# Attention scores behind the band in every second pair of units, and three score banks used in plain rotation

## The chip, the cores and the metric

The kernel runs on one core of a Trainium2 chip. The metric is the device time of one execution in microseconds (us); before the change it is 1020.58 us, the median of three runs (1019.04 to 1022.09).

## The reference, cut to what matters

One transformer layer, 8 sequences of 512 tokens, width 256, 16 heads of 16, in fp32:

```python
x = x + attention(layernorm(x))       # below
x = x + moe(layernorm(x))             # 7 routed experts, top 2, and 1 shared

q, k, v = shape(h @ Wq.T), shape(h @ Wk.T), shape(h @ Wv.T)      # (8, 16, 512, 16)
scores = einsum('bhqd,bhkd->bhqk', q, k) * SCALING + position_bias
ctx = einsum('bhqk,bhkd->bhqd', softmax(scores), v)
out = ctx @ Wo.T
```

`position_bias[h, q, k]` depends on k - q alone, and is constant where |k - q| is at least 91.

## The kernel before, in words

Three stages follow one another: `project` (q, k, v and the bias to HBM), `attend`, and `finish` (output projection, router and experts). The change lies in `attend`.

`attend` walks through 32 slots. A slot is one sequence and a group of four heads, and has 8 steps; a step is one pair of heads (two sides, on the upper and the lower half of the contraction rows) and one tile of 128 positions. Three streams of work are laid over each other on TensorE in each step of slot n:

- `scores` (line 740, tile pS): two matmuls of 512 columns, one for each side, each into a bank of pS. Each is a "unit"; a slot has 16. They are made 15 steps ahead of the exponents (`LEAD` = 7, plus a slot), only to find the row maxima. VectorE (line 680) adds the bias `near` to a unit and reduces it to its negated maximum in one instruction, followed by a short read of the accumulator that raises the semaphore `max_done`. A unit's bank is free again when `max_done` has counted it.
- `exponents` (line 757, tile pE): the scores once more, transposed, with the negated maximum and far bias as extra contraction rows, two matmuls of 512 columns; then eight short matmuls (line 765) that add the bias band of 154 to 244 columns. ScalarE (line 711) takes the exponent of two banks at once. pE has four banks, so steps alternate between two halves.
- `values` (line 779, tile pC): in every odd step, eight fp32 matmuls of the slot before's probabilities with v; `copy_ctx` (line 719) empties pC on ScalarE once a slot.

After the 16 units of a slot, `turn` (lines 687, 689, 693) splits and transposes the maxima on VectorE; GpSimd then sends them to HBM and back into the rows of `q_st` (lines 642 and 649), where the exponents of that slot read them. SyncE loads q, k, v, the far rows and, at the start of a group, the bias.

The order on TensorE is written out by hand in `slot` of `attend`: in each step `scores`, then `exponents`, then in odd steps `values`. Scores made in step s of a slot are those of step (s + 7) mod 8 of a later one, so an even step makes the units of an odd step, and the other way round. Write a and b for the two units of an even step of a slot, c and d for those of the odd step behind it, and a', b' for the next ones. The four units of such a pair of steps are what "pair" means below.

Three of pS's banks are used. Units go to places, and place modulo 3 is the bank; two places of each 18 (those before unit 6 and before unit 14) are left empty (`PLACES`). So most units wait for the unit three before them (line 739), units 6, 7, 14 and 15 for the one two before them, and units 8 and 0 for the one five before them (`held`). In regular places, d waits for a, a' for b, b' for c and c' for d.

Of the kernel before, what the change touches and what calls it, by code (L numbers as in the profile page):

```python
# [18 lines left out]
P = 128  # L19
B, S, D = 8, 512, 256  # L20
# [13 lines left out]
BIG = 3.0e38  # L34
# [15 lines left out]
def band_start(kh):  # L50

    return S - 1 - (FAR - 1) - (HALF - 1) - HALF * kh


def band(kh):

    return max(0, band_start(kh)), min(S, band_start(kh) + BW)
# [15 lines left out]
def raw(t):  # L73

    return t.bitcast(F32)
# [450 lines left out]
def attend(nc, mk, g):  # L526
# [5 lines left out]
    near, bandT, q_st, k_st, v_raw = (g[n] for n in ("near", "bandT", "q_st", "k_st", "v_raw"))  # L532
    near_ld, band_ld, qk_ld, far_ld, v_ld = (g[n] for n in ("near_ld", "band_ld", "qk_ld", "far_ld", "v_ld"))
    passed = g["passed"]
    with ExitStack() as ctx:
# [3 lines left out]
        sums = sb("sums", [P, 4, S], BF16)  # L539
# [4 lines left out]
        pS = ps("pS", [P, 3, S], F32)  # L544
        pE = ps("pE", [P, 4, S], F32)
        pC = ps("pC", [P, S], F32)
        s_mm, max_done, split_done, max_turned, max_out, max_ld = (sem(n) for n in (
            "s_mm", "max_done", "split_done", "max_turned", "max_out", "max_loaded"))
# [3 lines left out]
        PV0, MAX0 = 8, 4  # L552
# [1 line left out]
        STEPS = HPG // 2 * TT  # L554
        LEAD = 7

        PLACES = [*range(6), None, *range(6, 14), None, 14, 15]
        BANK = {unit: k % 3 for k, unit in enumerate(PLACES)}

        def held(unit):  # L560

            k = PLACES.index(unit) - 3
            while PLACES[k] is None:
                k -= 3
            return PLACES[k] + 1 - (16 if k < 0 else 0)

        def await_stores(engine):

# [4 lines left out]
        with nc.Block() as block:  # L573
# [90 lines left out]
            @block.vector  # L664
            def _(dve):
                dve.sem_inc(max_done, MAX0)  # L666

                def maxima(m, step):

                    hg = m // 8  # L670
                    pair, t = divmod(step, TT)
                    for side in range(2):
                        j, r = 2 * pair + side, 2 * step + side
                        if m % 8 == 0 and t == 0:
                            dve.wait_ge(near_ld[j], 16 * (hg + 1))
                        unit = 16 * m + r
                        dve.wait_ge(s_mm, unit + 1)
                        dve.wait_ge(max_done, MAX0 + unit - 3)
                        lead = P * t
                        dve.tensor_tensor_reduce(sums[:, r % 4], pS[:, BANK[r]], near[:, hg % 2, j, lead:lead + S], -1.0, BIG,  # L680
                                                 ALU.add, ALU.min,
                                                 nmax[:, j, t:t + 1]).then_inc(max_done, 1)

                def turn(m):

                    dve.wait_ge(max_done, MAX0 + 16 * m + 16)
                    dve.tensor_copy(nparts[:, 0], nmax[:]).then_inc(split_done, 1)
                    dve.wait_ge(split_done, 2 * m + 1)
                    dve.tensor_tensor(nparts[:, 1], nmax[:], nparts[:, 0], ALU.subtract).then_inc(split_done, 1)
                    dve.wait_ge(split_done, 2 * m + 2)  # L690
                    if m >= 2:
                        dve.wait_ge(max_out, 16 * m - 16)
                    dve.transpose(turned[:, m % 2], raw(nparts[:].rearrange("p a j t -> p (a j t)"))).then_inc(max_turned, 1)

                for ahead in range(STEPS * NI):
                    m, step = divmod(ahead, STEPS)
                    maxima(m, step)
                    if step == STEPS - 1:
                        turn(m)
                dve.wait_ge(den_ld, 16)  # L700
                dve.reciprocal(den[:], den[:]).then_inc(den_inv, 1)
# [24 lines left out]
            @block.tensor  # L726
            def _(pe):
                pe.sem_inc(pv_done, PV0)
                pe.wait_ge(g["rows_set"], 32)

                def scores(m, r, rounds, step):

                    pair, t = divmod(step, TT)
                    if step == 0:
                        pe.wait_ge(qk_ld[r], 16 * 8 * rounds)
                    for side in range(2):
                        unit = 2 * step + side
                        rows = slice(HALF * side, HALF * side + KQ)
                        pe.wait_ge(max_done, MAX0 + 16 * m + held(unit))
                        pe.matmul(pS[:, BANK[unit]], q_st[rows, r, pair, P * t:P * t + P], k_st[rows, r, pair],  # L740
                                  start=True, stop=True).then_inc(s_mm, 1)

                def exponents(n, r, step, quad, u, first):

                    pair, t = divmod(step, TT)
                    if u == 0 and t == 0 and quad % 2 == 0:
                        for side in range(2):
                            pe.wait_ge(band_ld[2 * pair + side], 16 * (quad // 2 + 1))
                    if step == 0:
                        pe.wait_ge(far_ld[r], 32 * (quad // 2 + 1))  # L750
                        pe.wait_ge(max_ld, 32 * (n + 1))
                    if not (first and step < 2):
                        pe.wait_ge(exp_done, STEPS * n + step - 1)
                    bank = 2 * (step % 2)
                    for side in range(2):
                        rows = slice(HALF * side, HALF * side + KS)
                        pe.matmul(pE[:, bank + side], k_st[rows, r, pair, P * t:P * t + P], q_st[rows, r, pair],  # L757
                                  start=True, stop=False, skip_group_check=True)
                    for half in range(2):
                        a, z = band(2 * t + half)  # L760
                        lead = a - band_start(2 * t + half)
                        for part in range(2):
                            for side in range(2):
                                rows = slice(HALF * side, HALF * side + HALF)
                                ins = pe.matmul(pE[:, bank + side, a:z], place[rows, half],  # L765
                                                bandT[rows, (quad // 2) % 2, pair, part, lead:lead + z - a],
                                                start=False, stop=half == 1 and part == 1, skip_group_check=True)
                    ins.then_inc(e_mm, 1)

                def values(n, par, t, first=False):  # L770

                    if t == 0:
                        pe.wait_ge(exp_done, STEPS * n + STEPS)
                        pe.wait_ge(v_ready, n + 1)
                        if not first:
                            pe.wait_ge(evac, n)
                    for j in range(HPG):
                        at = 8 * (j // 2) + 2 * t + j % 2
                        ins = pe.matmul(pC[32 * j:32 * j + 32], v_aug[:, par, t, j], prob[:, par, at],  # L779
                                        start=t == 0, stop=t == TT - 1, skip_group_check=True)  # L780
                    ins.then_inc(pv_done, 1)

                def slot(n, u, quad, first=False, last=False):
                    for step in range(STEPS):
                        ahead, other = divmod(STEPS + step + LEAD, STEPS)
                        if not (last and u + ahead > 3):
                            scores(n + ahead, (u + ahead) % 4, quad + 1 + (u + ahead) // 4, other)
                        exponents(n, u, step, quad, u, first and u == 0)
                        if step % 2 == 1 and not (first and u == 0):
                            values(n - 1, (u + 1) % 2, step // 2, first and u == 1)  # L790

                for step in range(STEPS + LEAD):
                    scores(step // STEPS, step // STEPS, 1, step % STEPS)
                for quad in range(QUADS):
                    for u in range(4):
                        slot(4 * quad + u, u, quad, first=quad == 0, last=quad == QUADS - 1)
                for t in range(TT):
                    values(NI - 1, 1, t)
# [488 lines left out]
```

## Time and profile before

| | us |
|---|---|
| median of 3 runs | 1020.58 |
| the profiled execution | 1021.6 |
| its span in the trace | 1019.8 |
| of it, slots 1 to 29 of attention | 391.56 |

The profiled execution is 1.8 us longer than its span, and 1.0 us longer than the median. TensorE is busy 95% of the span, VectorE 69%, ScalarE 50%. How to read the rows: a timeline row gives the start and the length of a merged group of instructions and, in brackets, the idle time before it and who ended it. PE is the matmul side of TensorE, PEld its loads of stationary operands. A matmul's wait is carried by its load, so PEld rows show who held it. The start of a matmul is recorded, its end is modelled; so the argument goes by starts.

### The profile page before, as it was taken

The numbers are of one execution on the slowest core, as the hardware profiler recorded it, in microseconds if no ns is written. First come the engines' busy times: TensorE is split into PE (matmuls) and PEld (weight loads), VectorE is DVE, ScalarE is ACT, GpSimd is POOL, SyncE is SP. The second block draws the span as 40 slices with busy tenths as digits, with TensorE's granted clock in tenths as the row PEclk, the third lists the DMA queues.
The fourth block names the chain that finished last, engine by engine and source line by source line (L and its number), as shares of the span: only waits on it lengthen the run. The fifth ranks groups of instructions, "written<-read, shape, count | busy, mean of one in ns | idle before, by whom it ended". The sixth has DMA issues, their size and how long they took to land. (4 is left out here: it accounts for less than half of the span.)

```text
span 1019.8 us, 20280 instructions
## 1 busy us (share of the span) xinstructions
PE 966.6 (95%) x7264; PEld 721.1 (71%) x7264; DVE 703.4 (69%) x2048; ACT 514.8 (50%) x680; POOL 109.4 (11%) x245
## 2 busy tenths in 40 slices
PE   5799599999999999999999499999999999999998
PEld 3688266666666666666665388888888798888887
DVE  5575587777787877777781667666666575766664
ACT  2344046666666666666667355444344334434433
POOL 2111021111111111111111100000000000000000
PEclk9899589999999999999999699999999999999999
DMA  4998864334543444333352411101111110101000
GB/s 115 303 342 282 240 136 125 104 95 120 132 115 105 125 136 127 86 94 93 87 156 80 134 42 52 60 25 43 41 42 43 41 41 21 62 1 42 1 22 21
DMA packets 65715, 100.27 MB, mean 98 GB/s; under 512 B 11256, under 2 KB 39440, under 8 KB 65598
## 3 DMA queue, kind: packets, MB, share of 16 engines
q1 hardware_dynamic: 62386, 97.49, 31.8%
q0 software_dynamic: 3072, 1.11, 1.0%
q8 instruction: 51, 0.84, 0.4%
q10 hardware_dynamic: 172, 0.56, 0.2%
q14 instruction: 34, 0.28, 0.1%
HBM read 63.67 MB, written 34.93 MB: 97 GB/s over the span
## 5 line engine op out<-in xcount | busy, mean ns | idle before, releaser
L680 DVE CUSTOM_DVE_ANT_0 sums<-pS,near 128x512 bf16<-128x512 f32 x512 | 324.8, 686 | 91.0 <-PE pS L740 90.7
L711 ACT ACTIVATE prob<-pE 128x1024 f32<-128x1024 f32 x256 | 261.3, 1025 | 173.4 <-PE pE L765 173.0
L1187 PE MATMUL pD<-w2p,h_p 128*128 128x256 f32 x1536 | 203.0, 285 | 1.8 <-DVE x L1037 1.8
L1187 PEld LDWEIGHTS pD<-w2p,h_p 128*128 128x128 f32 x1536 | 191.4, 188 | 11.2 <-DVE x L1037 2.6
L765 PEld LDWEIGHTS pE<-bandT,place 64*128 64x128 f32 x2048 | 183.6, 188 | 16.4
L1169 PE MATMUL pU<-x2T,w1p 128*128 128x512 f32 x768 | 191.7, 399 | 0.0
L1100 ACT ACTIVATE h_f<-pU,b1s 128x512 f32<-128x512 f32 x128 | 88.1, 688 | 191.8 <-PE pU L1169 185.9
L740 PE MATMUL pS<-k_st,q_st 48*128 48x512 f32 x512 | 171.8, 493 | 11.5 <-DVEq L666 7.7
L765 PE MATMUL pE<-bandT,place 64*128 64x244 f32 (+2 forms) x2048 | 181.8, 270 | 0.0
L740 PEld LDWEIGHTS pS<-k_st,q_st 48*128 48x128 f32 x512 | 75.3, 191 | 142.3 <-DVE nmax L680 132.3
L1169 PEld LDWEIGHTS pU<-x2T,w1p 128*128 128x128 f32 x768 | 141.6, 190 | 29.5
L1037 DVE SCALAR_TENSOR_TENSOR x<-pD,combine,x 128x256 f32<-128x256 f32 x256 | 110.8, 478 | 64.0 <-PE pD L1187 62.4
L757 PE MATMUL pE<-q_st,k_st 62*128 62x512 f32 x512 | 142.6, 423 | 0.0
L779 PE MATMUL pC<-prob,v_aug 128*32 128x512 f32 x1024 | 135.7, 604 | 1.0 <-ACT ctx_sb L719 1.0
L1026 DVE TENSOR_TENSOR h_p<-h_f,h_p 128x512 fp32r<-128x512 f32 x128 | 86.8, 690 | 68.0 <-ACT h_p L1103 65.6
L1103 ACT ACTIVATE h_p<-pU,b1s 128x512 fp32r<-128x512 f32 x128 | 87.2, 681 | 0.0
L757 PEld LDWEIGHTS pE<-q_st,k_st 62*128 62x128 f32 x512 | 61.4, 187 | 6.2 <-ACT prob L711 5.0
L472 PE MATMUL pQ<-xT,w_p 128*128 128x512 f32 x192 | 51.3, 420 | 7.8 <-DVE qk L390 5.8
L472 PEld LDWEIGHTS pQ<-xT,w_p 128*128 128x128 f32 x192 | 37.4, 203 | 19.6 <-DVE qk L390 9.9
L214 POOL TENSOR_SCALAR rtmp<-mv 128x4 f32<-128x4 f32 x16 | 5.8, 364 | 422.8 <-DVE mv L946 359.1
L649 POOL DMA_DIRECT2D q_st<-negated_maxima x64 | 34.8, 548 | 83.5 <-DMA negated_maxima<-turned 83.5
L680 DVE DVE_READ_ACCUMULATOR2_ANT nmax<- 128x1 f32 x512 | 42.4, 83 | 0.0
(102 smaller groups left out, 575.4 us busy)
## 6 DMA issues: line engine op xcount, KB each, us to landing
x<-in_x SPq DMA_DIRECT2D x16, 512.0 KB, 4.4
q_parts<-qk SPq DMA_DIRECT2D x16, 512.0 KB, 5.0
k_parts<-qk SPq DMA_DIRECT2D x16, 512.0 KB, 4.6
q_st<-q_parts SPq DMA_DIRECT2D x64, 128.0 KB, 2.8
k_st<-k_parts SPq DMA_DIRECT2D x64, 128.0 KB, 2.9
ctx<-ctx_sb SPq DMA_DIRECT2D x32, 256.0 KB, 2.7
near<-bias_by_distance SPq DMA_DIRECT2D x16, 448.0 KB, 5.7
v_rows<-vs SPq DMA_DIRECT2D x8, 512.0 KB, 3.4
```

The source lines that it names most:

```text
L472: ins = pe.matmul(pQ[:, m % 2], w_p[:, a, w, c, P * h:P * h + P], xT[:, par, z, c], start=k == 0, stop=k == 5)
L680: dve.tensor_tensor_reduce(sums[:, r % 4], pS[:, BANK[r]], near[:, hg % 2, j, lead:lead + S], -1.0, BIG, ALU.add, ALU.min, nmax[:, j, t:t ...
L711: act.activation(prob[:, par, 2 * step:2 * step + 2], pE[:, 2 * (step % 2):2 * (step % 2) + 2], ACT.Exp).then_inc(exp_done, 1)
L740: pe.matmul(pS[:, BANK[unit]], q_st[rows, r, pair, P * t:P * t + P], k_st[rows, r, pair], start=True, stop=True).then_inc(s_mm, 1)
L757: pe.matmul(pE[:, bank + side], k_st[rows, r, pair, P * t:P * t + P], q_st[rows, r, pair], start=True, stop=False, skip_group_check=True)
L765: ins = pe.matmul(pE[:, bank + side, a:z], place[rows, half], bandT[rows, (quad // 2) % 2, pair, part, lead:lead + z - a], start=False, st ...
L779: ins = pe.matmul(pC[32 * j:32 * j + 32], v_aug[:, par, t, j], prob[:, par, at], start=t == 0, stop=t == TT - 1, skip_group_check=True)
L1037: dve.scalar_tensor_tensor(out=row, in0=pD[:, t // 2, t % 2], scalar=combine[:, par, t, e:e + 1], in1=row, op0=ALU.mult, op1=ALU.add).then ...
L1100: act.activation(h_f[:, e % 2, m], pU[:, e % 2, m], ACT.Gelu, bias=b1s[:, e, m:m + 1])
L1103: act.activation(h_p[:, e % 2, 0, m], pU[:, e % 2, m], ACT.Gelu, bias=b1s[:, e, m:m + 1]).then_inc(s["h_hi"], 1)
L1169: ins = pe.matmul(pU[:, e % 2, m], w1p[:, e, a, c, P * m:P * m + P], x2T[:, par, c, z], start=k == 0, stop=k == 5)
L1187: ins = pe.matmul(pD[:, t2, u], h_p[:, e % 2, a, m, P * t:P * t + P], w2p[:, e, z, m], start=k == 0 and e < NE - 1, stop=k == 5)
```

## The change

`PLACES`, `BANK` and `held` go: unit u counted through all slots lies in bank u modulo 3, and waits for unit u - 3, always. In odd steps `scores` is issued behind `exponents` (and ahead of `values`); even steps keep their order. The line numbers of the new kernel are 8 or so smaller below the removed lines. No instruction is added or removed apart from that.

```diff
-        PLACES = [*range(6), None, *range(6, 14), None, 14, 15]
-        BANK = {unit: k % 3 for k, unit in enumerate(PLACES)}
-
-        def held(unit):
-
-            k = PLACES.index(unit) - 3
-            while PLACES[k] is None:
-                k -= 3
-            return PLACES[k] + 1 - (16 if k < 0 else 0)
+        PS = 3
...
-                        dve.tensor_tensor_reduce(sums[:, r % 4], pS[:, BANK[r]], near[:, hg % 2, j, lead:lead + S], -1.0, BIG,
+                        dve.tensor_tensor_reduce(sums[:, r % 4], pS[:, unit % PS], near[:, hg % 2, j, lead:lead + S], -1.0, BIG,
...
-                        unit = 2 * step + side
+                        unit = 16 * m + 2 * step + side
                         rows = slice(HALF * side, HALF * side + KQ)
-                        pe.wait_ge(max_done, MAX0 + 16 * m + held(unit))
-                        pe.matmul(pS[:, BANK[unit]], q_st[rows, r, pair, P * t:P * t + P], k_st[rows, r, pair],
+                        pe.wait_ge(max_done, MAX0 + unit + 1 - PS)
+                        pe.matmul(pS[:, unit % PS], q_st[rows, r, pair, P * t:P * t + P], k_st[rows, r, pair],
                                   start=True, stop=True).then_inc(s_mm, 1)
...
-                        if not (last and u + ahead > 3):
+                        early = step % 2 == 0
+                        if early and not (last and u + ahead > 3):
                             scores(n + ahead, (u + ahead) % 4, quad + 1 + (u + ahead) // 4, other)
                         exponents(n, u, step, quad, u, first and u == 0)
+                        if not early and not (last and u + ahead > 3):
+                            scores(n + ahead, (u + ahead) % 4, quad + 1 + (u + ahead) // 4, other)
```

## Rows read from the trace of the kernel before

**Rows 1.** The page's first part: busy us (share of the span) xinstructions of each engine.

```profile
PE 966.6 (95%) x7264; PEld 721.1 (71%) x7264; DVE 703.4 (69%) x2048; ACT 514.8 (50%) x680; POOL 109.4 (11%) x245
```

**Rows 2.** Stretches: us, busy of PE, PEld, DVE, ACT, POOL, PEclk, DMA share, GB/s.

```profile
106.20:136.90 30.70, 21.85 (x56) 11.22 (x58) 22.43 (x74) 1.13 (x2) 4.10 (x7) 0.50 0.92 223
...
144.93:536.49 391.56, 391.56 (x3714) 245.34 (x3715) 309.90 (x1015) 254.89 (x262) 62.78 (x116) 1.00 0.41 114
...
563.60:590.90 27.30, 15.04 (x53) 11.26 (x54) 19.80 (x60) 9.48 (x16) 2.68 (x8) 0.56 0.43 126
```

**Rows 3.** Waits in 144.93 to 536.49: us in total, times, longest us.

```profile
PEld pS L740 <- DVE nmax L680: 118.6, 231, 0.8
```

**Rows 4.** Timeline of PE, one pair of steps in slot 12: start, us, instruction.

```profile
303.17 0.50 PE L740 MATMUL pS<-k_st,q_st 48*128 48x512 f32 x2
303.51 0.40 PE L757 MATMUL pE<-q_st,k_st 62*128 62x512 f32 x2
303.74 0.61 PE L765 MATMUL pE<-bandT,place 64*128 64x244 f32 x8
304.19 0.76 PE L740 MATMUL pS<-k_st,q_st 48*128 48x512 f32 x2
304.46 0.72 PE L757 MATMUL pE<-q_st,k_st 62*128 62x512 f32 x2
304.80 0.79 PE L765 MATMUL pE<-bandT,place 64*128 64x218 f32 x8
305.52 1.07 PE L779 MATMUL pC<-prob,v_aug 128*32 128x512 f32 x8
306.52 0.50 PE L740 MATMUL pS<-k_st,q_st 48*128 48x512 f32 x2
```

**Rows 5.** Timeline of PEld, the waiting loads of the same pair.

```profile
303.16 0.19 PEld L740 LDWEIGHTS pS<-k_st,q_st 48*128 48x128 f32 x2 [0.84 <-DVE nmax L680]
...
304.46 0.18 PEld L740 LDWEIGHTS pS<-k_st,q_st 48*128 48x128 f32 x1 [0.19 <-DVE nmax L680]
```

**Rows 6.** Timeline of DVE, the eviction of unit a of the same pair.

```profile
303.70 0.69 DVE L680 CUSTOM_DVE_ANT_0 sums<-pS,near 128x512 bf16<-128x512 f32 x1 [0.87 <-PE pS L740]
304.32 0.08 DVE L680 DVE_READ_ACCUMULATOR2_ANT nmax<- 128x1 f32 x1
```

**Rows 7.** Timeline of PE in slots 30 and 31, where scores run out.

```profile
536.15 0.50 PE L740 MATMUL pS<-k_st,q_st 48*128 48x512 f32 x2
536.49 0.40 PE L757 MATMUL pE<-q_st,k_st 62*128 62x512 f32 x2
...
538.95 0.50 PE L757 MATMUL pE<-q_st,k_st 62*128 62x512 f32 x2
...
541.47 0.50 PE L757 MATMUL pE<-q_st,k_st 62*128 62x512 f32 x2
...
551.63 0.50 PE L757 MATMUL pE<-q_st,k_st 62*128 62x512 f32 x2
...
554.20 0.50 PE L757 MATMUL pE<-q_st,k_st 62*128 62x512 f32 x2
```

**Rows 8.** Timeline of DVE around the turn of a slot: b ends, then c.

```profile
308.28 0.08 DVE L680 DVE_READ_ACCUMULATOR2_ANT nmax<- 128x1 f32 x1
...
308.95 0.68 DVE L680 CUSTOM_DVE_ANT_0 sums<-pS,near 128x512 bf16<-128x512 f32 x1
309.55 0.08 DVE L680 DVE_READ_ACCUMULATOR2_ANT nmax<- 128x1 f32 x1
```

**Rows 9.** Timeline of DVE in the lead, at a unit behind an empty place.

```profile
116.58 0.69 DVE L680 CUSTOM_DVE_ANT_0 sums<-pS,near 128x512 bf16<-128x512 f32 x1 [0.27 <-PE pS L740]
```

**Rows 10.** Timeline of PE, the first exponents of slot 0.

```profile
133.41 0.80 PE L757 MATMUL pE<-q_st,k_st 62*128 62x512 f32 x2
```

**Rows 11.** Timelines of POOL in slot 13 and SP in slot 15: maxima back, last load.

```profile
312.38 1.09 POOL L649 DMA_DIRECT2D q_st<-negated_maxima x2 [2.36 <-DMA negated_maxima<-turned]
...
338.45 0.35 SPq L200 DMA_DIRECT2D v_raw<-v_rows  x1
```

## The prediction, made before the change was run

> **What bounds the kernel now.** I read the page's busy times first, then the stretches by stage, then the waits of the attention stage, then the timelines of one pair of steps. The page says TensorE: 95% busy [rows 1]. The stretches put 391.56 us on slots 1 to 29 of attention, at the full clock (1.00, the 2.4 GHz level), with TensorE busy in every microsecond [rows 2]. That is 391.56 / 29 = 13.50 us a slot, 3.375 us a pair of steps. "Busy" is too kind, though: a matmul's end is modelled, and a row can cover a stall. The waits say that loads for pS stood idle for VectorE 118.6 us in 231 cases, two a pair [rows 3]. The timeline shows the two kinds. One is 0.84 us at the first scores of a pair, the other 0.19 us at unit d [rows 5].
>
> The 0.84 us one is no wait for VectorE. It spans the `values` matmuls, and stands in the same length where nothing can be waited for: from values to the next work is 306.52 - 305.52 = 1.00 us [rows 4], most of it the fp32 matmuls themselves. The 0.19 us one is real. Unit d needs the bank of a. Unit a's matmul starts at 303.17, its eviction at 303.70 (0.535 us later); the accumulator read that raises `max_done` starts at 304.32 and takes 0.083 us [rows 6]; d's load starts at 304.46 [rows 5]. So a bank comes back 0.535 + 0.616 + 0.083 + 0.055 = 1.29 us after its matmul when VectorE is free. But d could have run beside c at 304.19. While d is held, so are the exponents behind it in TensorE's order: exponents to band takes 304.80 - 304.46 = 0.34 us where the unheld one takes 303.74 - 303.51 = 0.23 us, the loads of the sides drift apart and no longer pair up, and values start only at 305.52 [rows 4].
>
> What would a pair cost without the stall? Slots 30 and 31 show it, since there scores run out. A pair without scores takes 541.47 - 538.95 = 2.52 us (long band, then short) or 554.20 - 551.63 = 2.57 us (short, then long), 2.545 on average [rows 7]. One pair of score matmuls costs 0.235 us: from the last scores to the next pair is 538.95 - 536.15 = 2.80 us, 0.23 above 2.57 [rows 7], the same as an unheld exponent pair [rows 4]. So 2.545 + 2 x 0.235 = 3.015 us a pair, 12.06 us a slot. The stall costs 3.375 - 3.015 = 0.36 us a pair.
>
> **The change part by part.** *Scores of odd steps behind the band.* No instruction is added; the work of c and d is 0.235 us in either place. Take a's matmul as 0. Even step: scores to exponents 0.34 (536.15 to 536.49) [rows 7], exponents and band 0.68 (303.51 to 304.19, the long band, the dearer one) [rows 4]; odd step the same at most, 0.68. So c and d now start at about 1.70 instead of 1.02, and a's bank is back at 1.29. The stall of d goes whole, with 0.4 us to spare. Whatever c and d are moved past is on TensorE itself: the exponents and band of the odd step come 0.235 us plus the stall earlier, so ScalarE gets that step earlier. It can take it: it is busy 254.89 / 29 = 8.8 us a slot [rows 2], of 12.2.
>
> *What is late next: b'.* b' needs the bank of c. c starts at 1.70, is evicted from 1.70 + 0.535, and its bank is back at 1.70 + 1.29 = 2.99. TensorE reaches a' and b' at 3.03 in such a pair (2.57 + 0.47); in the other (2.52) both shrink together. So b' finds its bank with 0.04 us to spare: no stall, but next to nothing in hand. a' needs b, back at about 1.90; c' needs d; d' needs a'. VectorE evicts one unit every 0.61 us (303.70 to 304.32) [rows 6], so 2.45 us a pair; a and b run 0.54 to 1.76, c and d 2.24 to 3.47, and a' is ready at 3.03 + 0.54 = 3.57. It keeps up, with 0.1 us of slack where it had 0.9.
>
> A rule of the Trainium skill speaks against that last step. VectorE: DVE Perf Modes, section "The DRAIN you can't avoid", says that a VectorE instruction's successor doesn't start before the pipe is empty, though it also lets those that are not held start earlier. The trace disagrees with the strict reading for this instruction: 0.69 us long, the next one 0.61 us behind it.
>
> *Regular banks.* The two empty places a slot go. Their units waited for the one two before them; that cost VectorE 0.27 us of idle time each in the lead, where scores run alone [rows 9]. In the 15 steps of the lead there are four such places: up to 4 x 0.27 = 1.1 us gained, or nothing where a load of q and k ends last there instead. The price is at the turn: it takes VectorE from 308.28 to 308.95, 0.67 us between b and c [rows 8]. c's eviction can then start at 1.76 + 0.67 = 2.43 instead of 2.24. The read is 0.60 later [rows 8], so b's successor b' gets its bank at 2.43 + 0.60 + 0.084 + 0.055 = 3.17 against 3.03: a stall of 0.14 us once a slot. Before, the wait for the unit five back kept c' out of this. Between nothing (if it is made up in the band) and 0.36 (if it upsets the pairing as d's 0.19 does now), I take 0.14, the plain delay.
>
> *Slot 0* has no values, so TensorE has only 2 us of work a pair there and the loop c to b' binds: 2.99 us a pair. It now takes from 133.41 [rows 10] to 144.93 [rows 2], 2.88 us a pair, so some 0.5 us more in sum. With the lead's gain I book nothing for the two, within 1 us. Part of it runs at the 1.2 GHz level (0.50 until 136.90) [rows 2]. Slots 30 and 31 have no scores to move.
>
> *Queues.* SyncE and GpSimd get no new order, only shorter slots. The reload of the maxima starts at 312.38 and takes 1.1 us to issue [rows 11]; it lands by about 316 and is wanted at the next slot's start, 320.0 now, 318.7 then. SyncE's last load of a slot is issued 5 us into it (338.45; the slot began at 333.5) [rows 11], and is wanted over a slot later. Neither ends last. `finish` is untouched; its start at the mixed clock (0.56) [rows 2] may move 2 us either way, as the clock's steps fall differently on it.
>
> **Sum.** A slot 4 x 3.015 + 0.14 = 12.20 us against 13.50: 1.30 x 29 = 37.7 us. Profiled execution 1021.6 - 37.7 = 983.9. The median of the runs stands 1.0 below the profiled one: 982.9, so 983.
>
> **The rivals.** *(1) The stall moves to b'.* The 0.04 us in hand is less than what I can read off sums of rows. If the loop closes 0.1 to 0.15 us late, or the disturbance costs double its wait as at d now, a pair takes about 3.14 us, a slot 12.7: 23 us gained, 997. For: the thin margin. Against: c's place was taken at the dearer band.
> *(2) VectorE becomes the bound.* If its real interval between units were the instruction and the read one after the other, 0.69 + 0.08 = 0.77 us, a pair would need 3.08 us and the turn 0.67 more a slot: 13.0 us, 15 us gained, 1005. Against: it keeps 0.61 in every row that I read. The Trainium skill's page named above, read strictly, would give this.
> *(3) Slower.* One mechanism: c issued late makes b' late on top of a stall that stays at d. It would be a pair of 3.015 + 2 x 0.36 = 3.73 us, a slot 14.9, 41 us lost: 1062. It decides from the point where c gives its bank back more than 0.4 us later than worked out (2.99 + 0.39 = 3.38), so that the new stall outweighs the old one; each 0.1 us beyond costs 11.6 us. Against: a's own bank comes back in 1.29 by row, and c's is the same work.
> *(4) It does nothing.* If the 0.36 us a pair is no stall but a cost of four score matmuls among the others, reordering leaves it: 1020. Against: the 0.19 us row and the drifting sides.
>
> **How the numbers follow.** Forecast 0.72; (1) 0.12; (2) 0.04; (4) 0.05; (3) 0.07. The forecast's own bounds: no cost of the turn (0.14 x 29 = 4 us), 1 us from the lead and 2 from the clock give 976; the turn at 0.36 and the clock against me give 992. To leave out no more than 2 in 10 the range reaches to the middle of rival 1 and a little past it: 976 to 1000. A difference of 0.3% (3 us) is about what a measurement of this kernel tells from no change. Faster: 0.72 + 0.12 + 0.04 = 0.88; same 0.05; slower 0.07.
>
> **What would show it right or wrong.** Right: slots of 12.2 us between 144 and 500; scores c and d as a row of two in one piece, 1.7 us after a and b, with values 0.33 us behind; no 0.19 us idle row at a pS load in the plain pair, and one of about 0.14 once a slot; exponent to band 0.23 us in odd steps. Rival 1: a short pS load wait in every pair, at its second load. Rival 2: VectorE without gaps. Wrong altogether: a slot still at 13.5 with no waiting load, or the exponents waiting for the maxima or for ScalarE at a slot's start.

## The result, and the profile after

The changed kernel takes 989.01 us, the median of four runs (985.09 to 991.38), against 1021.11 before (1019.04 to 1022.09, four runs): a ratio of 0.968, 95% interval 0.965 to 0.972. The forecast was 983 (976 to 1000), a ratio of 0.963. The profiled execution took 985.09, its span 983.3. No TensorE, VectorE or ScalarE instruction came or went; the page's busy line, which answers to [rows 1], shows 35.5 us of TensorE's "busy" gone, which in the main was stall under the modelled ends:

```profile
PE 931.1 (95%) x7264; PEld 695.4 (71%) x7264; DVE 708.1 (72%) x2048; ACT 501.3 (51%) x680; POOL 109.4 (11%) x245
```

The stretches of after (columns as in [rows 2]): the stretch at the low clock, slot 0, slots 1 to 29, and the start of `finish`.

```profile
106.63:140.76 34.13, 26.19 (x79) 14.58 (x79) 23.93 (x81) 3.79 (x4) 5.59 (x10) 0.50 0.78 205
...
132.62:146.38 13.76, 12.28 (x96) 10.05 (x97) 9.06 (x32) 7.57 (x8) 2.19 (x4) 0.70 0.31 83
...
146.38:502.20 355.82, 355.81 (x3713) 219.13 (x3715) 315.58 (x1016) 242.07 (x262) 62.79 (x116) 1.00 0.44 126
...
529.88:550.36 20.48, 9.88 (x38) 7.21 (x38) 14.09 (x30) 6.68 (x12) 2.62 (x6) 0.58 0.50 154
```

Slots 1 to 29 took 355.82 / 29 = 12.27 us each instead of 13.50: 35.7 us gained. The rest of the span: slot 0 began 0.8 us earlier (first exponents at 132.62, before 133.41), slot 0 took 13.76 us instead of 11.52 (2.2 lost), and what follows slot 29 took 983.3 - 502.20 = 481.1 instead of 1019.8 - 536.49 = 483.3 (2.2 gained; `finish` started with 20.48 us at 0.58 of the full clock, where [rows 2] has 27.30 at 0.56). Sum 36.5 = 1019.8 - 983.3.

One plain pair of after on TensorE (timeline, slot 14), to be laid beside [rows 4]:

```profile
311.71 0.50 PE L732 MATMUL pS<-k_st,q_st 48*128 48x512 f32 x2
312.05 0.40 PE L749 MATMUL pE<-q_st,k_st 62*128 62x512 f32 x2
312.28 0.60 PE L757 MATMUL pE<-bandT,place 64*128 64x154 f32 x8
312.72 0.41 PE L749 MATMUL pE<-q_st,k_st 62*128 62x512 f32 x2
312.96 0.62 PE L757 MATMUL pE<-bandT,place 64*128 64x244 f32 x8
313.42 0.39 PE L732 MATMUL pS<-k_st,q_st 48*128 48x512 f32 x2
313.74 1.07 PE L771 MATMUL pC<-prob,v_aug 128*32 128x512 f32 x8
314.74 0.50 PE L732 MATMUL pS<-k_st,q_st 48*128 48x512 f32 x2
```

Both exponents now run to their band in 0.23 to 0.24 us, where the second one took 0.34 before; c and d start at 313.42, 1.71 us behind a and b; values follow 0.32 us later; the pair takes 3.03 us. The weight loads of the same stretch (PEld, in brackets the idle time before), and VectorE at c:

```profile
308.51 0.36 PEld L732 LDWEIGHTS pS<-k_st,q_st 48*128 48x128 f32 x2 [0.84 <-issue]
...
311.71 0.19 PEld L732 LDWEIGHTS pS<-k_st,q_st 48*128 48x128 f32 x2 [0.84 <-DVE nmax L672]
...
313.31 0.19 PEld L732 LDWEIGHTS pS<-k_st,q_st 48*128 48x128 f32 x2
...
314.73 0.19 PEld L732 LDWEIGHTS pS<-k_st,q_st 48*128 48x128 f32 x2 [0.84 <-DVE nmax L672]
```

```profile
313.94 0.69 DVE L672 CUSTOM_DVE_ANT_0 sums<-pS,near 128x512 bf16<-128x512 f32 x1 [0.39 <-issue]
314.56 0.08 DVE L672 DVE_READ_ACCUMULATOR2_ANT nmax<- 128x1 f32 x1
```

The 0.19 us wait of [rows 5] is gone from c and d (313.31, no bracket). c's accumulator read ends at 314.56 + 0.08 = 314.64, and the loads of a' and b' go at 314.73: b' had its bank about 0.04 us before it was wanted, once the 0.055 us from semaphore to load is counted. The 0.84 us brackets stay, as they must: they span the values. The row at 308.51 is the other case, the turn. It covers two loads in 0.36 us instead of 0.19: b' went 0.18 us after a'. VectorE says why; its turn ended so late that c was evicted from 307.94 and read at 308.55, and b's successor could not load before 308.69. Of the 29 turns, 24 have such a row of 0.32 to 0.34 us, so about 0.15 us of delay; three have 0.18, one 0.10, and one, at 480, has 0.50, behind an eviction for whose start the trace names no releaser. VectorE at the turn of 308:

```profile
307.94 0.69 DVE L672 CUSTOM_DVE_ANT_0 sums<-pS,near 128x512 bf16<-128x512 f32 x1
308.55 0.08 DVE L672 DVE_READ_ACCUMULATOR2_ANT nmax<- 128x1 f32 x1
```

### The profile page after: what moved, and what is told of

Read it like the earlier page. It is cut to its first block and busy times, and to the rows that moved or that the text cites. A ratio compares the mean times of both kernels' runs of the same rounds, so it can differ in the third digit from the quotient of the medians.

```text
span 983.3 us, 20280 instructions
## 1 busy us (share of the span) xinstructions
PE 931.1 (95%) x7264; PEld 695.4 (71%) x7264; DVE 708.1 (72%) x2048; ACT 501.3 (51%) x680; POOL 109.4 (11%) x245
## 5 line engine op out<-in xcount | busy, mean ns | idle before, releaser
L672 DVE CUSTOM_DVE_ANT_0 sums<-pS,near 128x512 bf16<-128x512 f32 x512 | 329.2, 687 | 52.0 <-PE pS L732 43.8
L703 ACT ACTIVATE prob<-pE 128x1024 f32<-128x1024 f32 x256 | 248.4, 1021 | 152.3 <-PE pE L757 152.2
L1164 PE MATMUL pU<-x2T,w1p 128*128 128x512 f32 x768 | 189.5, 396 | 0.0
L757 PEld LDWEIGHTS pE<-bandT,place 64*128 64x128 f32 x2048 | 166.3, 190 | 12.2
L757 PE MATMUL pE<-bandT,place 64*128 64x244 f32 (+2 forms) x2048 | 163.5, 272 | 0.0
L732 PE MATMUL pS<-k_st,q_st 48*128 48x512 f32 x512 | 139.8, 477 | 10.7 <-DVEq L658 7.6
L732 PEld LDWEIGHTS pS<-k_st,q_st 48*128 48x128 f32 x512 | 64.1, 193 | 120.0 <-DVE nmax L672 86.6
L749 PE MATMUL pE<-q_st,k_st 62*128 62x512 f32 x512 | 114.6, 403 | 0.9 <-DMA q_st<-negated_maxima 0.9
L749 PEld LDWEIGHTS pE<-q_st,k_st 62*128 62x128 f32 x512 | 57.5, 189 | 7.3 <-ACT prob L703 5.0
L771 PEld LDWEIGHTS pC<-prob,v_aug 128*32 128x32 f32 x1024 | 20.7, 108 | 32.3 <-issue 29.6
```

The source lines that it names most:

```text
L672: dve.tensor_tensor_reduce(sums[:, r % 4], pS[:, unit % PS], near[:, hg % 2, j, lead:lead + S], -1.0, BIG, ALU.add, ALU.min, nmax[:, j, t: ...
L703: act.activation(prob[:, par, 2 * step:2 * step + 2], pE[:, 2 * (step % 2):2 * (step % 2) + 2], ACT.Exp).then_inc(exp_done, 1)
L732: pe.matmul(pS[:, unit % PS], q_st[rows, r, pair, P * t:P * t + P], k_st[rows, r, pair], start=True, stop=True).then_inc(s_mm, 1)
L1164: ins = pe.matmul(pU[:, e % 2, m], w1p[:, e, a, c, P * m:P * m + P], x2T[:, par, c, z], start=k == 0, stop=k == 5)
```

## The experiments

All were timed or profiled beside the kernel before on the same chip (1023.34 us for the first four, 1022.95 for the others). The theory was the bank loop: a bank of scores is back 1.29 us after its matmul, and where that falls later than TensorE's order wants the bank, the pair is longer. The main rivals were that the order alone, or the banks alone, or mere distance between the score pairs, brought the gain; and that the 0.36 us a pair was no stall.

**The order alone.** The kernel before, with only the last hunk of the change:

```diff
+                        early = step % 2 == 0
-                        if not (last and u + ahead > 3):
+                        if early and not (last and u + ahead > 3):
...
+                        if not early and not (last and u + ahead > 3):
```

> The order of the change (odd steps' scores behind the band) with the empty places of before. Theory of the bank loop: d's stall of 0.36 us a pair goes, but in two of the four pairs of a slot b' waits for d instead of c (units 6, 7, 14, 15 wait for the unit two before them). d's bank is back at 2.24 + 0.61 + 0.61 + 0.14 = 3.60 us against 3.03: 0.57 us stalled in each of the two, and about 0.17 at the turn as after. Slot 12.06 + 1.14 + 0.17 = 13.4 us, so about 1017 us, nearly no change. Rival, that the order alone is what gains (the empty places cost little, as in the lead): slot 12.3, about 988 us.

Measured 1012.57 us (1009.24 to 1014.76) against 1023.34, ratio 0.989 (0.986 to 0.992). A slot is 378.64 / 29 = 13.06 us, between the two expectations and nearer to the loop's:

```profile
151.26:529.90 378.64, 378.64 (x3713) 227.56 (x3714) 318.88 (x1016) 241.92 (x261) 63.02 (x116) 1.00 0.41 118
```

Its weight loads, first behind the turn and then where units 6 and 7 are a' and b':

```profile
310.83 0.18 PEld L740 LDWEIGHTS pS<-k_st,q_st 48*128 48x128 f32 x2 [0.84 <-DVE nmax L680]
...
313.86 0.18 PEld L740 LDWEIGHTS pS<-k_st,q_st 48*128 48x128 f32 x1 [0.84 <-DVE nmax L680]
314.33 0.18 PEld L740 LDWEIGHTS pS<-k_st,q_st 48*128 48x128 f32 x1 [0.29 <-DVE nmax L680]
```

b' goes 0.47 us after a', since it waits for d and not for c. The place is the one forecast, and there are just two of them a slot (58 held second loads in slots 1 to 29). The size was forecast as 0.57; c's eviction starts 2.13 us after the load of a there (312.96 - 310.83), not 2.24. The third term of the forecast, 0.17 at the turn, did not come: the two loads behind the turn go together. With the floor of 12.13 us that is measured below, 12.13 + 2 x 0.47 = 13.07 us, which is the slot.

**The banks alone.** The changed kernel with the order of before (`scores` ahead of `exponents` in every step):

```diff
-                        if early and not (last and u + ahead > 3):
+                        if not (last and u + ahead > 3):
...
-                        if not early and not (last and u + ahead > 3):
```

> Plain rotation of the three banks with the order of before. Theory of the bank loop: d still waits for a, 0.36 us a pair, nothing else changes in the slots: 13.5 us a slot; about 1 us less in the lead: 1020 us. Rival, that the empty places were what cost: slot near 12.3, about 988 us.

Measured 1019.87 us, ratio 0.997 (0.996 to 0.998). The slots are as before, 391.92 / 29 = 13.51 us, and unit d is held as in [rows 5]:

```profile
144.35:536.27 391.92, 391.92 (x3714) 245.50 (x3715) 310.47 (x1017) 255.73 (x262) 62.81 (x116) 1.00 0.40 114
```

```profile
307.12 0.19 PEld L732 LDWEIGHTS pS<-k_st,q_st 48*128 48x128 f32 x1
307.50 0.18 PEld L732 LDWEIGHTS pS<-k_st,q_st 48*128 48x128 f32 x1 [0.19 <-DVE nmax L672]
```

So the parts bring 11 and 3 us alone and 33 together on this chip. In the slots, which the theory is about, it is 13.50 - 13.06 = 0.44 us, nothing, and 13.50 - 12.27 = 1.23 us each. The 3 us of the banks alone do not lie there: about 1 was expected of the lead, and the profiled execution (1022.27 us, the longest of the six) does not show where the rest is. The order removes the wait of d, but with the empty places it makes a new one; only the plain rotation lets b' wait for c, which is back in time.

**The changed kernel again**, unchanged:

> The changed kernel once more, beside the others on one chip. Slots 12.25 us and a ratio near 0.966 by both theories. If the runs spread over 6 us again, the profile should show the difference ahead of slot 1 or behind slot 31 (clock steps), not in the slots.

Measured 990.57 us (987.84 to 992.71), ratio 0.968 (0.965 to 0.970). The steady slots were the same, 12.27 us, but this execution had the low clock until 155.98:

```profile
108.19:155.98 47.79, 38.14 (x154) 24.36 (x158) 32.41 (x108) 10.15 (x10) 6.29 (x11) 0.50 0.66 159
135.04:151.76 16.72, 15.26 (x96) 12.60 (x97) 9.02 (x30) 8.11 (x8) 2.19 (x4) 0.50 0.24 54
151.76:166.08 14.32, 14.32 (x130) 9.12 (x131) 11.34 (x37) 8.15 (x10) 1.88 (x4) 0.85 0.46 112
```

Slots 0 and 1 took 16.72 + 14.32 = 31.0 us, against 26.2 in the first profile of after and 24.9 before. Of the 7.6 us between the two profiled executions of the changed kernel, 4.9 lie there, 2.4 ahead of slot 0 (it began at 135.04, not 132.62), and 0.3 behind. For the other six executions only the time and the mean granted clock are on record; the clock falls by and large as the time grows, from 0.969 at 985.09 us to 0.963 at 992.71.

**Behind the values.** The changed kernel, with the odd steps' `scores` moved once more, behind `values`:

```diff
                         exponents(n, u, step, quad, u, first and u == 0)
-                        if not early and not (last and u + ahead > 3):
-                            scores(n + ahead, (u + ahead) % 4, quad + 1 + (u + ahead) // 4, other)
                         if step % 2 == 1 and not (first and u == 0):
                             values(n - 1, (u + 1) % 2, step // 2, first and u == 1)
+                        if not early and not (last and u + ahead > 3):
+                            scores(n + ahead, (u + ahead) % 4, quad + 1 + (u + ahead) // 4, other)
```

> As the changed kernel, but the odd steps' scores stand behind the values too. Theory of the bank loop: c starts at 2.70 us instead of 1.70, its bank is back 1.29 later, at 3.99, and b' waits for it: a pair 3.99 us, a slot 16.0, some 2.5 x 29 = 72 us over before: 1092 us. Rival, that the gain comes from anything that stands between the two score pairs (spacing them): slot 12.3 or less, about 988 us.

Measured 1104.88 us, ratio 1.080 (1.078 to 1.082). TensorE in one pair, then VectorE at c:

```profile
327.08 0.50 PE L732 MATMUL pS<-k_st,q_st 48*128 48x512 f32 x1 [0.56 <-DVE nmax L672]
...
329.88 0.73 PE L732 MATMUL pS<-k_st,q_st 48*128 48x512 f32 x3
331.17 0.50 PE L732 MATMUL pS<-k_st,q_st 48*128 48x512 f32 x1 [0.56 <-DVE nmax L672]
```

```profile
330.41 0.69 DVE L672 CUSTOM_DVE_ANT_0 sums<-pS,near 128x512 bf16<-128x512 f32 x1 [0.88 <-PE pS L732]
331.02 0.08 DVE L672 DVE_READ_ACCUMULATOR2_ANT nmax<- 128x1 f32 x1
```

c starts at 329.88, b' at 331.17, 1.29 us later to the hundredth, and TensorE stands still for 0.56 us in each pair: 331.17 - 327.08 = 4.09 us. That is 0.10 us more than the 3.99 expected, since c comes 2.80 us behind the pair's start (at b') and not 2.70; over the 116 pairs of slots 1 to 29 it is 12 us, most of the distance from 1092 to 1105. Moving the scores one stage too far costs more than the first move brought. Distance as such gains nothing.

**Half an eviction.** VectorE reads 256 of the 512 columns in the kernel before (half the keys are left out of the maxima); TensorE's work is untouched:

```diff
-dve.tensor_tensor_reduce(sums[:, r % 4], pS[:, BANK[r]], near[:, hg % 2, j, lead:lead + S], -1.0, BIG,
+dve.tensor_tensor_reduce(sums[:, r % 4, 0:S // 2], pS[:, BANK[r], 0:S // 2], near[:, hg % 2, j, lead:lead + S // 2], -1.0, BIG,
```

> The kernel before, with VectorE reading only the first 256 of the 512 columns of each unit (half of the keys are left out of the maxima); TensorE's work is the same. Theory of the bank loop: an eviction takes about 0.35 instead of 0.61 us, a's bank is back at 1.02 instead of 1.29, so d is held for 0.1 us at most: a pair 3.02 to 3.12 us, a slot 12.1 to 12.5. Rival, that four score matmuls in that order cost TensorE 0.36 us more whatever VectorE does: 13.5 us.

One run, 987.7 us. The slots fell to 348.33 / 28 = 12.44 us with the order and the banks of before:

```profile
154.24:502.57 348.33, 348.33 (x3586) 233.11 (x3584) 187.51 (x980) 243.27 (x253) 61.07 (x113) 1.00 0.44 124
```

```profile
304.20 0.51 PE L740 MATMUL pS<-k_st,q_st 48*128 48x512 f32 x2
304.44 0.50 PE L757 MATMUL pE<-q_st,k_st 62*128 62x512 f32 x2
304.67 0.72 PE L765 MATMUL pE<-bandT,place 64*128 64x244 f32 x8
305.32 1.06 PE L779 MATMUL pC<-prob,v_aug 128*32 128x512 f32 x8
```

The exponents reach their band in 0.23 us again. So the stall was one on VectorE's release, not a cost of TensorE's order: a faster eviction removes three quarters of it. That VectorE's reads as such slow TensorE is ruled out by the changed kernel, which reads all 512 columns and takes 3.03 us a pair. The rest, (12.44 - 12.13) / 4 = 0.08 us a pair, is what a small hold at d leaves; its load goes 0.11 us after c's. In the kernel before it goes 0.38 us after c's, of which the row shows 0.19 as idle, since c's load fills the other half. The two kernels, half eviction first:

```profile
304.10 0.30 PEld L740 LDWEIGHTS pS<-k_st,q_st 48*128 48x128 f32 x2
```

```profile
304.08 0.18 PEld L740 LDWEIGHTS pS<-k_st,q_st 48*128 48x128 f32 x1
```

**Half an eviction in the changed kernel**, the same edit on its line:

```diff
-dve.tensor_tensor_reduce(sums[:, r % 4], pS[:, unit % PS], near[:, hg % 2, j, lead:lead + S], -1.0, BIG,
+dve.tensor_tensor_reduce(sums[:, r % 4, 0:S // 2], pS[:, unit % PS, 0:S // 2], near[:, hg % 2, j, lead:lead + S // 2], -1.0, BIG,
```

> The changed kernel with the same half eviction. Theory: the stall of about 0.17 us at the turn goes, a slot is 12.06 to 12.1 us, the four pairs alike; slots 0 and 1, where the loop of c and b' binds at the lower clock, get shorter by about 0.25 us a pair. Rival for the turn (its 0.17 us is a cost on TensorE): the slot stays at 12.25.

One run, 984.08 us. 339.57 / 28 = 12.13 us a slot, 4 x 3.03: what was held at the turn, 0.14 us, is gone. This is the floor of TensorE's work, forecast as 12.06. The second expectation, shorter slots 0 and 1, is not borne out. At the low clock a pair of slot 0 did get shorter, from 4.14 to 3.88 us (from one held load to the next, 136.74 to 140.88 and 138.03 to 141.91), but slot 0 took 14.78 us, where the changed kernel took 13.76 in one profile and 16.72 in the other, and the clock rose only at 147.2, between their 140.76 and 155.98. One run can't tell whether the shorter holds moved it.

```profile
134.18:148.96 14.78, 14.19 (x97) 11.71 (x97) 5.35 (x27) 7.45 (x8) 1.99 (x4) 0.56 0.29 78
161.32:500.89 339.57, 339.57 (x3586) 203.69 (x3584) 189.87 (x980) 234.10 (x253) 61.08 (x113) 1.00 0.44 127
```

**Slot 0 in the old order.**

```diff
-                        early = step % 2 == 0
+                        early = step % 2 == 0 or (first and u == 0)
```

> The changed kernel, with the order of before in slot 0 alone, where there are no values. Theory of the clock: with the new order the loop of c and b' binds in slot 0, TensorE stands idle in each pair and the half clock lasts longer (to 140.8 us in one profile and 156.0 in the other, against 136.9 before), which costs 2 to 8 us and makes the spread of 6 us. Slots 0 and 1 together go back to about 24 us (11.2 + 12.6) from 26.2 and 31.0, the clock is full from about 137 us: 983 to 985 us, spread 3 us or less. Rival, that the late clock comes from the lead, which is 1 us shorter with plain rotation: the clock still rises at 140 or later, 987 to 991 us.

Measured 985.06 us (984.45 to 986.35, five runs), ratio 0.965 (0.962 to 0.967).

```profile
106.56:137.28 30.72, 23.40 (x68) 13.46 (x70) 23.46 (x78) 2.05 (x2) 4.10 (x7) 0.50 0.86 222
132.20:143.59 11.39, 11.28 (x97) 10.02 (x98) 10.61 (x36) 7.49 (x8) 2.19 (x4) 0.78 0.41 105
143.59:155.78 12.19, 12.19 (x129) 7.42 (x130) 10.97 (x36) 8.55 (x10) 1.88 (x4) 1.00 0.48 132
```

The clock is back at 137.28, as before, and slots 0 and 1 take 23.6 us instead of 26.2 and 31.0. The spread falls from 5 or 6 us to 2. The ratio to the kernel before falls from 0.968 to 0.965, 3 to 4 us; the intervals (0.965 to 0.970, 0.962 to 0.967) overlap, and the runs were on two chips. The lead kept its plain rotation, so the late clock came with the order in slot 0. The other profiles agree. With the old order in slot 0 the clock rose between 136.7 and 138.4 in all five (before, banks alone, half eviction before, this one, the next one); with the new order it rose at 140.76, 145.3, 147.2, 149.99 and 155.98. The order alone, in the banks of before:

```profile
105.62:149.99 44.37, 34.46 (x126) 20.90 (x126) 29.00 (x95) 7.46 (x8) 5.59 (x10) 0.50 0.64 165
```

What in that order does it is not shown. The expectation names the idle of the held loads, but no run takes that away and keeps the order; with the half eviction it was shorter, and the clock still rose late.

**The turn split.** On top of that, the transposition of the maxima goes behind units 0 and 1 of the next slot, with two buffers of maxima:

```diff
+        nmax = sb("nmax", [P, 2, HPG, TT], F32)
...
                     if step == STEPS - 1:
                         turn(m)
+                        if m in (0, NI - 1):
+                            transpose(m)
+                    if step == 0 and m >= 2:
+                        transpose(m - 1)
```

> As slot0_old, and the last third of the turn (the transposition) is made behind units 0 and 1 of the next slot, where VectorE has a gap, with two buffers of maxima. Theory: c's eviction starts 0.13 to 0.2 us earlier at the turn, b' is no longer held: a slot 12.06 to 12.1 us, 4 to 5 us less than slot0_old, less what the maxima cost that now come 1.3 us later (in 3 of 29 slots they had less than that in hand). Rival, that the later maxima hold the exponents at each slot's start: as slot0_old or slower.

Measured 983.15 us (980.88 to 983.21, five runs), ratio 0.962 (0.960 to 0.964): 2 us less than its base, where 4 to 5 were expected. VectorE at the turn, and the longer of the two places where the maxima came too late:

```profile
291.55 0.18 DVE L681 TENSOR_TENSOR nparts<-nmax,nparts 128x16 fp32r<-128x16 f32 x1
291.67 0.69 DVE L672 CUSTOM_DVE_ANT_0 sums<-pS,near 128x512 bf16<-128x512 f32 x1
...
292.89 0.21 DVE L688 STREAM_TRANSPOSE turned<-nparts 128x32 f32<-128x32 f32 x1
```

```profile
485.64 0.50 PE L756 MATMUL pE<-q_st,k_st 62*128 62x512 f32 x2 [1.52 <-issue]
```

b' is no longer held: all 112 pairs of slots 2 to 29 have their two loads together. But the maxima land later by the time of two evictions, and TensorE stood still for 1.52 us at the first exponents of slot 29 and for 1.13 at 241.00. The rows name no releaser; the last transfer of the maxima to `q_st` was issued at 480.2 and took 5.2 to 5.4 us to land, which is 485.6 and fits. The same 28 slots, first the base:

```profile
155.78:499.42 343.64, 343.64 (x3586) 211.12 (x3584) 304.39 (x981) 233.76 (x253) 60.90 (x113) 1.00 0.44 126
```

```profile
155.05:497.87 342.82, 340.17 (x3587) 203.84 (x3584) 303.48 (x982) 234.05 (x253) 61.08 (x113) 1.00 0.45 126
```

Busy time fell by 343.64 - 340.17 = 3.5 us, 0.12 a slot, and 342.82 - 340.17 = 2.65 us of idle came back. So the slots gained only 0.8 us; of the 3.6 us between the two profiled executions most lies elsewhere, 2.1 of it behind slot 29, and the 2 us of the medians are not shown to be the turn's.

## Why the prediction was right, point by point

- *The stall in the kernel before, 0.36 us a pair.* Right in kind, and nearly in size. The half eviction showed it as a wait on the bank. The floor of a slot was 12.13 (3.03 us a pair) against the 12.06 (3.015) worked out from slots 30 and 31, so the stall was (13.50 - 12.13) / 4 = 0.34 us, and the slots gained 35.7 us where 37.7 were forecast.
- *c and d at 1.70 us, the bank back 1.29 us later, b' with 0.04 us in hand.* Right to 0.01: 1.71 in after; 1.29 where b' does wait, behind the values; about 0.04 left. Rival 1 rested on that margin and didn't come in any plain pair. The waits count 89 held loads in slots 1 to 29, 73.8 us, against 118.6 in 231 [rows 3]. All but two are brackets over the values (one of the two is at the turn at 480, the other at the end of slot 0):

```profile
PEld pS L732 <- DVE nmax L672: 73.8, 89, 0.8
```

- *The turn, 0.14 us.* Right in place and size: b' about 0.15 us late in 24 of 29 turns, 12.27 - 12.13 = 0.14 us a slot. Slots forecast at 12.20, measured 12.27.
- *VectorE keeps 0.61 us a unit.* Right, rival 2 fell: 313.94 to 314.56. The Trainium skill's page VectorE: DVE Perf Modes, section "The DRAIN you can't avoid", read strictly, would by an estimate from the rows have put 0.69 + 0.08 = 0.77 there; the section itself lets an instruction that is not held start earlier.
- *Slower, rival 3.* It fell for the change, but half of its mechanism exists: b' waits for c, while no stall stays at d. With c 1.0 us later than in the change the loop closes at 4.09 us a pair, and the kernel is 8% slower. The point from which it turns, 3.375 us a pair, lies between.
- *Slot 0 and the lead, booked at nothing within 1 us.* Wrong. The forecast had the loop bind in slot 0 at 2.99 us a pair, at about the speed of before. At the full clock that held: 2.66 to 2.74 us, where before took 2.66 on average (136.95 to 144.93). At the 1.2 GHz level it did not: a pair of the old order takes 3.55 us there, one of the new order 4.1 to 4.2, and the clock stays at that level until 140.76 or 155.98 instead of 136.90 [rows 2]. Slots 0 and 1 took 26.2 and 31.0 us in the two profiles, 2.6 and 7.5 over the 23.6 of the kernel with slot 0 in the old order. That kernel's ratio is 0.965, near the 0.963 of the forecast.
- *The clock behind attention, 2 us either way.* It came to 2.2 us in favour in the profiled execution. This was covered by the range but not by the number.
- *The number.* For the profiled execution the sum was 983.9, and 985.09 was measured. This is closer than its terms: the slots gained 2.0 us less, slot 0 with its start lost 1.4, and the clock behind attention gave 2.2 back, which was luck. The median was put 1.0 us below the profiled execution, as before; it came 3.9 above it, since the profiled one was the shortest of the four. These 4.9 us are the larger part of the 6 by which the forecast missed.

## What to carry to other kernels

Where a producer and a consumer rotate through few banks, write down for each producing instruction which release it waits for, and when that release falls in the period: moving an instruction changes two gaps, the one before it and the one behind it, and the best place is where both are just covered (here the loop is 1.29 us, and in a period of 3.03 us d comes 1.71 us behind a, and b' 1.32 us behind c; no place in between was tried). Order and buffer assignment are one decision: alone they brought 11 and 3 us, together 33. And look at the first round apart, since work that hides the loop in the steady state may be missing there.

## What the runs showed of the hardware that was not expected

- *A modelled "busy" hides stalls.* TensorE was busy 391.56 of 391.56 us before, and 35.7 us of that could go without an instruction less.
- *A late second load costs about as much as it is late.* The two sides' loads for pS normally go together. Where the second went 0.11, 0.15, 0.38 and 0.47 us after the first (half eviction before, the turn, d before, b' in the order alone), the slot grew by 0.08, 0.14, 0.34 and 0.47 us for each such place. The idle bracket shows less of it: 0.19 us for the 0.38 at d.
- *The clock at the start of attention depends on the order in slot 0.* In five profiles with the new order it was at the 1.2 GHz level until 140.76 to 155.98; these two ends are executions of one and the same kernel. In slot 0 of the later one TensorE's rows still show it busy 15.26 of 16.72 us. With the old order there it rose between 136.7 and 138.4 in five. Why was not found.
